# First attention of a four-layer network in the form of the fourth, with four of thirteen key tiles masked after the exponential

## The reference, cut to what matters

```python
q, k, v = split_heads(Q @ Wq.T + bq), split_heads(K @ Wk.T + bk), split_heads(V @ Wv.T + bv)
scores = einsum('bhqd,bhkd->bhqk', q, k) / sqrt(8)
L0: scores = scores + mask * -1e9          # float mask, 1.0 is masked
L3: masked scores are replaced             # int32 mask, 0 is masked
out = merge_heads(softmax(scores) @ v) @ Wo.T + bo
```

## Time and profile before

| | us |
|---|---|
| median of 3 runs (2112.62 to 2113.97) | 2113.92 |
| profiled execution, its own time | 2117.23 |
| its span, first to last instruction | 2115.5 |

### The profile page before, as it was taken

One profiled execution on the slowest core, in us unless ns is written; L12 is line 12 of the kernel. 1 busy time (PEld: TensorE's weight loads), 2 busy tenths in 40 slices (PEclk: granted clock), 3 DMA queues, 4 the chain that ended last, 5 costly groups with the idle time before them and its releaser, 6 DMA issues. The chain is left out here.

```text
span 2115.5 us, 43716 instructions
## 1 busy us (share of the span) xinstructions
PE 1917.5 (91%) x17178; PEld 1359.3 (64%) x17178; DVE 1298.4 (61%) x3213; ACT 1300.2 (61%) x2097; POOL 134.0 (6%) x347
## 2 busy tenths in 40 slices
PE   6999999967868659999999999999995699999997
PEld 4677777744634537777777777777774466666664
DVE  6888888877445235455555554555555776666663
ACT  4999999955357125555555555555564466666664
POOL 4000000000122110000000000000000400000000
PEclk9999999987878679999999999999997789999998
DMA  6211111102170510000000000000000621111110
GB/s 235 57 46 43 47 43 47 43 16 76 37 198 4 156 44 2 1 2 1 1 2 1 1 1 1 2 1 1 1 2 1 209 57 43 47 43 46 47 38 17
DMA packets 55307, 87.71 MB, mean 41 GB/s; under 512 B 9881, under 2 KB 31437, under 8 KB 55105
## 3 DMA queue, kind: packets, MB, share of 16 engines
q1 hardware_dynamic: 54593, 83.87, 13.4%
q0 software_dynamic: 512, 1.05, 0.2%
HBM read 66.93 MB, written 17.96 MB: 40 GB/s over the span
## 5 line engine op out<-in xcount | busy, mean ns | idle before, releaser
L2438 ACT ACTIVATE a_prT<-bank 128x512 f32<-128x512 f32 (+1 forms) x448 | 232.7, 565 | 328.6 <-PE bank L2347 328.4
L1181 DVE CUSTOM_DVE_ANT_0 a_attn_junk<-wide,a_mask 128x801 f32<-128x801 f32 (+1 forms) x256 | 247.5, 991 | 123.2 <-PE wide L1011 123.1
L1122 ACT ACTIVATE a_attn_prT<-bank 128x512 f32<-128x512 f32 (+1 forms) x448 | 237.2, 566 | 122.9 <-PE bank L1028 110.5
L2493 DVE CUSTOM_DVE_ANT_0 a_sc<-wide,a_zeros 128x1024 f32<-128x1024 f32 (+1 forms) x256 | 243.1, 988 | 87.3 <-PE wide L2333 87.3
L1478 DVE CUSTOM_DVE_ANT_0 a_attn_sc<-wide,a_mask 128x801 f32<-128x801 f32 (+1 forms) x256 | 253.0, 989 | 11.6 <-PE wide L1327 9.9
L1343 PE MATMUL bank<-ident,a_attn_sc 128*128 128x128 f32 x1664 | 244.2, 275 | 15.3 <-ACT a_attn_prT L1435 14.1
L1343 PEld LDWEIGHTS bank<-ident,a_attn_sc 128*128 128x128 f32 x1664 | 198.6, 141 | 62.2 <-issue 42.3
L2347 PE MATMUL bank<-ident,a_sc 128*128 128x128 f32 x1664 | 231.3, 277 | 1.5 <-ACT a_prT L2438 1.5
L2347 PEld LDWEIGHTS bank<-ident,a_sc 128*128 128x128 f32 x1664 | 185.2, 140 | 54.4 <-issue 28.1
L2399 PEld LDWEIGHTS bank<-a_prT,a_vt 128*64 128x64 f32 x3328 | 180.3, 137 | 48.4 <-issue 47.0
L2333 PE MATMUL wide<-a_kT,a_qT 64*128 64x512 f32 (+1 forms) x1024 | 211.0, 529 | 0.0
(11 more groups left out here) (449 smaller groups left out, 2550.2 us busy)
## 6 DMA issues: line engine op xcount, KB each, us to landing
a_ks<-a_k_parts SPq DMA_DIRECT2D x384, 75.0 KB
a_k_parts<-a_proj_kp SPq DMA_DIRECT2D x24, 416.0 KB, 4.5
a_qx<-a_q_stack SPq DMA_DIRECT2D x384, 12.0 KB
moe_w1b<-in_e_w SPq DMA_DIRECT2D x15, 256.0 KB
ctxT<-in_ctxT SPq DMA_DIRECT2D x4, 832.0 KB, 10.6
a_ctxn<-in_ctxn SPq DMA_DIRECT2D x4, 832.0 KB, 7.1
m_q_stack<-m_proj_qp SPq DMA_DIRECT2D x9, 256.0 KB
m_ks<-m_k_parts SPq DMA_DIRECT2D x24, 96.0 KB
```

The source lines that it names most:

```text
L1122: act.activation(prT[0:keys, u % PRT, kt:kt + m, :], bank_of(s, f"W{g}")[0:keys, 0:m * S].rearrange("p (t q) -> p t q", q=S), ACT.Exp).the ...
L1181: dve.tensor_tensor_reduce(junk[:, n % 2, 0:w], S_WIDE[n % 2][:, 0:w], mask(qt, at, w), 1.0, LOWEST, ALU.add, ALU.max, mx[:, p % 2, qt, e, ...
L2438: copy = lambda out, src: act.activation(out, src, ACT.Copy)
L2493: dve.tensor_tensor_reduce(sc[:, s % 2, h, at:at + w], S_WIDE[h][:, 0:w], zeros[:, 0:w], 1.0, LOWEST, ALU.add, ALU.max, mx[:, s % 2, h, p: ...
```

## The change

- L0 uses `quad_attention_stage` too; `row_quad_stage` is gone. L0 gets the turned mask as a new input (mask0T, 1664 x 256 f32), the padding loads, six operand slots in place of four, and its weight rounding at step LAST-2 = 69 of DVE's loop, with PE's sum at the start of step 70.
- In both layers the turned groups 0 and 1 (key tiles 0 to 3) are computed without the mask matmul. Their exponents are masked afterwards: DVE takes, for tiles 0 and 1, the minimum with a tile that is 2^100 where valid and 0 where masked; POOL, for tiles 2 and 3, takes the minimum with 2^100 and multiplies by a tile of ones and zeros. The values of a quad wait for both.
- A row of queries whose keys are all masked is found at the start: 13 matmuls on PE at step 1, four operations on DVE.
- The K parts of the last block stay in SBUF, in what becomes the sixth prT slot. SP stores them in the attention, after the operands of unit 1, and DVE waits for that store at step 2.

The core of the diff (the removed `row_quad_stage` and lists of names are left out):

```diff
+CAPPED_TILES = 4
+CAP = 2.0 ** 100
...
@@ quad_attention_stage
-        prT = core.sb(ctx, name + "_prT", [P, PRT, KT, S], F32)
+        prT = core.sb(ctx, name + "_prT", [P, PRT - 1, KT, S], F32)
...
+        def probs(u):
+            return last_prT if u % PRT == PRT - 1 else prT[:, u % PRT, :, :]
...
                 load_operands(sp, b, h, u % RING, loaded[u % RING])
+                if u == LOADED_AHEAD:
+                    store_last(sp)
+            if weights:
+                sp.wait_ge(turned, NG * (UNITS - 2))
+                sp.dma_start(weights[0], weights[1]).then_inc(w_in, 16)
...
+                if g == 0 and u == 0:
+                    pe.wait_ge(flagged, 3)
...
-                    pe.matmul(out, core.identb[:, 0:keys], maskT(kt + j), start=True, stop=False)
-                    ins = pe.matmul(out, ks[0:MAX_ROW + 6, u % RING, at:at + keys], qx[0:MAX_ROW + 6, u % RING, :], start=False, stop=True)
+                    if g >= CAPPED:
+                        pe.matmul(out, core.identb[:, 0:keys], mask_rows(kt + j), start=True, stop=False)
+                    ins = pe.matmul(out, ks[0:MAX_ROW + 6, u % RING, at:at + keys], qx[0:MAX_ROW + 6, u % RING, :],
+                                    start=g < CAPPED, stop=True)
...
                 pe.wait_ge(exp_done, NG * (4 * q + 3) + (last - 1) // 2 + 1)
+                pe.wait_ge(capped, 4 * q + 4)
+                pe.wait_ge(weighed, 2 * (4 * q + 4))
...
+            def count_valid():
+                pe.wait_ge(setup, 2)
+                for kt in range(KT):
+                    ins = pe.matmul(BANKS[2][:, 0:S], counts[:, int(kt in (2, 3)), :],
+                                    cap[:, kt, :] if kt < CAPPED_TILES else mask_rows(kt), start=(kt == 0), stop=(kt == KT - 1))
+                ins.then_inc(flagged, 1)
...
+                if s == 1:
+                    count_valid()
+                if s == LAST - 1 and weights:
+                    sum_weights()
...
@@ POOL
+            def weigh_masked(u):
+                pair = probs(u)[:, 2:4, :]
+                if u == 0:
+                    pool.wait_ge(flagged, 5)
+                pool.wait_ge(exp_done, NG * u + 2)
+                pool.tensor_scalar(pair, pair, CAP, None, ALU.min).then_inc(weighed, 1)
+                pool.wait_ge(weighed, 2 * u + 1)
+                pool.tensor_tensor(pair, pair, cap[:, 2:4, :], ALU.mult).then_inc(weighed, 1)
+
+            for s in range(LAST):
+                if pair_rows(s) is not None:
+                    cut_maximum(pair_rows(s))
+                if 0 <= s - TURN < UNITS:
+                    weigh_masked(s - TURN)
...
@@ DVE
+                dve.wait_ge(exp_done, NG * u + 1)
+                dve.tensor_tensor(probs(u)[:, 0:2, :], probs(u)[:, 0:2, :], cap[:, 0:2, :], ALU.min).then_inc(capped, 1)
+
+            def flag_all_masked():
+                dve.wait_ge(flagged, 1)
+                for i, given in enumerate((1.0, 1.0 / CAP)):
+                    dve.tensor_scalar(alone[:, i, :], BANKS[2][:, 0:S], ALL_MASKED, given, ALU.is_le, ALU.mult).then_inc(flagged, 1)
+                dve.wait_ge(flagged, 3)
+                for i in range(2):
+                    dve.tensor_tensor(cap[:, 2 * i:2 * i + 2, :], cap[:, 2 * i:2 * i + 2, :],
+                                      alone[:, i:i + 1, :].broadcast_to([P, 2, S]), ALU.max).then_inc(flagged, 1)
...
                 maximum(s, 0)
+                if s == 2:
+                    dve.wait_ge(last_stored, 16 * 3)
+                    dve.memset(last_prT[:, KT - 1, :], 0.0).then_inc(setup, 1)
                 maximum(s, 1)
+                cap_masked(s)
                 maximum(s, 2)
                 normalise(s)
                 maximum(s, 3)
+                if s == 1:
+                    flag_all_masked()
+                if s == LAST - 2 and weights:
+                    quantise_weights()
...
@@ project_stage, SP
-            for i in range(blocks):
-                if i == blocks - 1:
-                    sp.wait_ge(q_stored, 16 * 3)
-                    sp.wait_ge(k_stored[0], 16 * len(k_rows(0)))
-                    load_first(sp)
+            for i in range(blocks - 1):
                 for rows, j in k_rows(i):
                     sp.wait_ge((part1, part2, part3)[j], n_ck * (i + 1))
                     sp.dma_start(rows, kp[:, i, j, :]).then_inc(k_stored[i], 16)
-            for i in range(blocks):
+            sp.wait_ge(k_stored[0], 16 * (3 + len(k_rows(0))))
+            load_first(sp)
+            for i in range(1, blocks - 1):
                 sp.wait_ge(k_stored[i], 16 * len(k_rows(i)))
...
@@ masked_head_layer
+        def store_last(sp):
+            for i in range(3):
+                sp.dma_start(k_parts[B - 1, :, i, :, :], k_last[:, i, :]).then_inc(k_stored[B - 1], 16)
...
+                ahead += [(seenT[:, :, :], inp["mask0T"].rearrange("(t p) q -> p t q", p=P), mask_in)] + pads
...
+            mask_work = [[], [conversion(maskT[:, :, :], seenT[:, CAPPED_TILES:, :], is_masked, MASKED, first=True)],
+                         [conversion(cap[:, 0:2, :], seenT[:, 0:2, :], is_valid, CAP),
+                          conversion(cap[:, 2:4, :], seenT[:, 2:4, :], is_valid, 1.0),
+                          conversion(mask[:, 0, :], seen[:, 0, :], is_masked, MASKED)],
+                         [conversion(mask[:, 1, :], seen[:, 1, :], is_masked, MASKED)]]
```

More of the change, by code:

```diff
@@ L950, in quad_attention_stage @@
         outT = core.sb(ctx, name + "_outT", [P, S], F32)
+        counts = core.sb(ctx, name + "_counts", [P, 2, P], BF16)
+        alone = core.sb(ctx, name + "_alone", [P, 2, S], BF16)
+        part = core.sb(ctx, name + "_part", [P, 3], F32)
+        inv = core.sb(ctx, name + "_inv", [P, 3], F32)
         block = ctx.enter_context(nc.Block())
@@ L1088, in output, with sum_weights @@
                 ins.then_inc(out_ready, 1)
+            def count_valid():
[4 more added lines that the diff above has]
+                ins.then_inc(flagged, 1)
+            def sum_weights():
+                pe.wait_ge(w_chain, 1)
+                pe.wait_ge(drained, 4 * UNITS)
+                pe.matmul(S_WIDE[0][:, 0:3], core.ones[:, :], part[:, :], start=True, stop=True).then_inc(w_chain, 1)
             for s in range(LAST):
+                if s == 1:
+                    count_valid()
+                if s == LAST - 1 and weights:
+                    sum_weights()
                 values(s)
@@ L1117, in exponent @@
                 if g == 0:
-                    act.wait_ge(setup, 2)
+                    act.wait_ge(setup, 5 if u >= PRT - 1 else 4)
                     if u >= PRT:
@@ L1152, in _, with cut_maximum @@
             pool.wait_ge(cut, 1)
-            for p in range(UNITS // 2):
+            def cut_maximum(p):
                 c = p % 2
@@ L1187, in maximum, with cap_masked, quantise_weights @@
                     dve.tensor_reduce(nmx[:, p % 2, :, :], mx[:, p % 2, :, :, :], X, ALU.max, negate=True).then_inc(max_ready, 1)
+            def cap_masked(s):
+                u = s - TURN
+                if not 0 <= u < UNITS:
+                    return
+                if u == 0:
+                    dve.wait_ge(flagged, 4)
+                dve.wait_ge(exp_done, NG * u + 1)
[8 more added lines that the diff above has]
+                                      alone[:, i:i + 1, :].broadcast_to([P, 2, S]), ALU.max).then_inc(flagged, 1)
+            def quantise_weights():
+                raw, raw_dram, wq, mean = weights
+                link = Link(dve, w_chain)
+                dve.wait_ge(w_in, 16)
+                link(dve.tensor_reduce(part[:, :], raw, X, ALU.add, apply_absolute_value=True))
+                link.n += 1
+                dve.wait_ge(w_chain, link.n)
+                link(dve.tensor_scalar(mean, S_WIDE[0][:, 0:3], 1.0 / (FF0 * D), 1e-5, ALU.mult, ALU.max))
+                link(dve.reciprocal(inv[:, :], mean))
+                for i in range(3):
+                    ins = dve.tensor_scalar(raw[:, i, :], raw[:, i, :], inv[:, i:i + 1], ROUND, ALU.mult, ALU.add)
+                link(ins)
+                link(dve.tensor_scalar(raw, raw, ROUND, 1.0, ALU.subtract, ALU.min))
+                link(dve.tensor_scalar(wq, raw, -1.0, None, ALU.max))
             def normalise(s):
@@ L1541, in project_stage @@
-def project_stage(core, name, w, bias, scale, src, src_in, ck, k_rows, q_rows, vs, load_first, row=None, mask_work=(), ahead=()):
+def project_stage(core, name, w, bias, scale, src, src_in, ck, k_rows, q_rows, vs, last, k_stored, load_first, row=None, mask_work=(), ahead=()):
     nc = core.nc
@@ L1567, in part @@
             i, c = n // n_ck, n % n_ck
-            return kp[:, i, j, c * ck:(c + 1) * ck]
+            return last[:, j, c * ck:(c + 1) * ck] if i == blocks - 1 else kp[:, i, j, c * ck:(c + 1) * ck]
         def left(n):
@@ L1751, in masked_head_layer, with conversion @@
                 ahead.insert(2, (mask[:, :, :], inp["mask0"].rearrange("(t p) k -> p t k", p=P), mask_in))
```

(18 more changed lines are left out.)

356 lines of the change are left out of this document (42 added, 314 removed).

## The result

The changed kernel takes 2125.53 us (median of 5 runs, 2124.16 to 2126.96) against 2113.92 for the kernel before (5 runs, 2112.62 to 2115.22). The ratio is 1.0053, 95% interval 1.0042 to 1.0064: slower by 11.6 us. The same kernel in a later series (5 runs, expected 1.0053 within 0.001) gave 2124.49 us and a ratio of 1.0054 (1.0041 to 1.0068). The forecast was 2149, so the sign was right and the size three times too large.

The account below looks back on a forecast made before the run. PE was taken as the bound, but DVE and POOL would take back its saving: L3 +11.3 and L0 +23.4, together +34.7 on the profiled 2117.2, less that execution's 3.3 above the median, gives 2149 us, range 2095 to 2180.

Parts of the forecast that it names:

- the quad after, followed: Attention, four steps traced through PE, DVE and POOL: a quad becomes 24.9 in place of 24.13 us, +12.3 a layer.
- POOL's minimum at 0.70: POOL's added one-input operation on each unit, taken as 0.70 us, with a range of 0.5 to 1.16.
- The waits of 0.94, 0.4 and 0.5 us: In each quad, DVE's minimum and POOL's two operations exclude one another, costing these three waits.
- All sixteen quads charged alike: Attention: +0.77 us for each of 16 quads, together +12.3 a layer.
- B's fourth maximum: DVE, in the quad's step B, which has no values: this maximum starts at 20.05 us after the quad's values start.
- D at 7.07: The quad's step with the first chunk of values: 7.52 less 0.45 us, its DVE work hidden.
- the start at +3.5 in L3: Start of the attention: DVE's added operations, PE's 13 matmuls and the three stores cost +3.5 us, between 2 and 5.5.
- The padding loads: L0's layer norm: these loads hold SP behind context and masks, +8 us, at most 11.5.
- The end of L0's projection: Idle time before the attention shrinks where no store has to land: 5.6 us gained in L0.
- the first (2067): PE stays the bound, DVE and POOL keep up: quad 22.35, -28.5 us a layer, 2067 us; chance 0.17.
- The second (2109, at a quad of 23.6): DVE and POOL miss each other, no waits: quad about 23.6, -8 us a layer, 2109 us; chance 0.15.
- The third had both its conditions met: POOL is dearer, minimum at 1.16 or more, loads late by their upper bound: quad 25.4, 2172 us; chance 0.15.

Follow-up runs that it names:

- e5: Changed kernel with POOL's two operations swapped, product ahead of minimum; 2141.39 us, one run only.
- run 16: Not a run number: "the one run 16 us" means e5's single run, about 16 us above the changed kernel, at 2141.39 us.
- e4: Changed kernel with tiles 8 to 11 masked afterwards in place of 0 to 3, DVE's minima and POOL's pair moved to other steps; 2089.30 us, ratio 0.9875.
- e6: Changed kernel with all thirteen mask matmuls a unit back on PE, no masking afterwards and no test for fully masked rows; 2126.11 us.
- e10: Changed kernel with only the three K stores and DVE's wait for them moved later, to unit 3 and step 6; 2125.96 us, ratio 1.0057.
- e1: Changed kernel with L0's three padding loads issued at the start of the projection instead of in the layer norm; 2119.91 us, ratio 1.0024.
- e8: Changed kernel with late masks (tiles 8 to 11), L0's padding loads moved to the projection and counted apart, weight rounding moved; 2071.71 us, ratio 0.9793.

## Why the prediction was wrong in size

The failed steps are in "the quad after, followed", whose +0.77 a quad and +12.3 a layer were measured as +0.15 and +0.1.

1. **POOL's minimum at 0.70.** It is 1.484. I had reasoned that one input makes it cheap and put it near DVE's 0.48; POOL's own rows pointed the other way, and the upper end of 1.16, from its product, was too low as well. By itself this error made the forecast too fast: the run without the minimum shows 0.79 a quad for 1.48 us.
2. **The waits of 0.94, 0.4 and 0.5 us between DVE and POOL.** The exclusion exists, but I let every moment of both POOL operations shut DVE out. The one-input operation does so only at its beginning, and since it is long, the product comes later, after DVE's minimum. In the changed kernel DVE is held in none of 128; 28 of 128 products are held, for 0.4. Where the order is turned (e5) and both engines are held more, a quad costs 0.48 more, and the one run 16 us. This error, the larger, made the forecast too slow. The place of the waits, on which it rests, depended on the mis-sized term above.
3. **All sixteen quads charged alike.** The three quads with an output projection gained 0.95 each in place of losing 0.77. That is 3 x 1.72 = 5.2 of the 12.2 us missed in a layer, against 10 x 0.62 = 6.2 from the ordinary quads.

The first two can be read off one quad of the changed kernel, whose values start at 1849.56 (PE's, DVE's and POOL's timelines):

```profile
1849.56 0.40 PE L1078 MATMUL bank<-a_attn_prT,a_vs 128*9 128x256 f32 x3 [0.72 <-POOL a_last_slot L1214]
...
1868.56 0.98 DVE L1238 CUSTOM_DVE_ANT_0 a_attn_junk<-wide,a_mask 128x800 f32<-128x800 f32 x1
...
1872.54 1.16 POOL L1214 TENSOR_TENSOR a_attn_prT<-a_attn_prT,a_cap 128x512 f32<-128x512 f32 x1
```

B's fourth maximum starts at t = 1868.56 - 1849.56 = 19.00, where I had 20.05: the waits of 0.94 and 0.4 aren't there, less a wait of 0.3 for the third piece. POOL's minimum is 0.78 longer than I took. The wait of 0.5 ahead of the product isn't there either. 24.9 - 1.05 + 0.78 - 0.5 = 24.13, and the product ends at 1872.54 + 1.16, t = 24.14; the values follow 0.14 later. So the waits made 1.55 too much and the minimum 0.78 too little, and that the quad's miss is only 0.62 is in part luck: two errors against each other.

For the third, PE's timeline of a quad with an output projection shows where the chain finds room:

```profile
1918.74 0.39 PE L1048 MATMUL bank<-a_qx,a_ks 102*128 102x256 bf16 x2 [0.83 <-DVE x L1314]
...
1922.73 0.40 PE L1078 MATMUL bank<-a_attn_prT,a_vs 128*9 128x256 f32 x3 [0.24 <-POOL a_last_slot L1214]
```

PE has the projection's work besides and waits for DVE's addition, and the values that follow wait 0.24 for POOL in place of 0.72. In e4, where PE is full, a projection adds 24.26 - 22.73 = 1.53 to a quad; in the changed kernel only 0.34. My reading is that DVE and POOL catch up meanwhile; no run takes the projection away. L3's quads came out at +0.1 for +12.3, L0's attention at -0.1 for +13.4: 25.7 of the 27.2 us by which the sum missed the span's +7.5, and 24.4 of them in the quads of the two layers.

What held: PE is no longer the bound (busy share 0.945); the values' wait for POOL once a quad and the score pieces' for DVE; D at 7.07; the start at +3.5 in L3 (3.7 measured; each of two causes is worth about 3 alone, 2.9 for the stores in e6 and 3.5 for the counting in e10, and both together no more), while L0's was 2.2; the gain of 2.4 from L0's form; L3's projection (-4.5 forecast, -5.1 measured); the rounding at +5.9. The padding loads reached their upper bound, +11.9 in place of +8. The end of L0's projection held too: the idle time before the attention went from 7.01 to 1.23 (the mark at 57.90), 5.8 for my 5.6, and the stage as a whole gained 3.7 for my 3.9. That, though, is so only because it began late: begun at 15.47 or 15.08 (e1, e8) its first mask conversion waits 4 us for its loads, and the stage takes 34.44 or 33.39, against 34.65 before. The forecast had no term for that wait, and in the changed kernel the late start hides it. Together L0 came out at +8.2 until the attention for +4.1.

Of the rivals, the first (2067) failed for where the work was put and not for how much there is: with the masks late PE is the bound again (297.71 busy of 300), though at 22.73 a quad and 2089 us, not at 22.35 and 2067. The second (2109, at a quad of 23.6) had the right mechanism and the wrong price of POOL. The third had both its conditions met, POOL's minimum above 1.16 and the loads at their upper bound, and still its 2172 was far off, since it kept the waits.

## What to carry to other kernels

Work moved from a full engine to idle ones is free only at the steps where they are idle: operations of the same kind and size cost 1.93 us a quad where they stood in the steps in which DVE keeps pace with PE (24.28 against the 22.35 of a PE that never waits), and 0.38 where they stood beside the values (22.73). Bound an operation that has no row by its own engine's rows and leave the upper end open; and before two waits are added or a cause is moved, ask whether another of the same size lies behind it, as the stores did behind the counting.

## What the runs showed of the hardware that I had not expected

- POOL's minimum with a constant, one input, 128x512 f32: 1.484 us; its product of two inputs of the same size: 1.158. The one-input operation is the slower.
- DVE's two-input operation and POOL's hold each other, whichever starts second, if it starts soon enough after the other. POOL's product shuts DVE out for about 1.03 of its 1.16 us, its one-input operation for about 0.46 of its 1.48 (each worked out from the rows above, at two offsets each).
- The queue took the loads of context and mask in some 0.4 to 0.7 us each and then held SP for 11.47 us over two small ones (10.36 and 10.89 us with these issued a stage later, e1 and e8).
